# Other start addresses for the operands of the split float32 matmuls in a cross-attention and FFN block

## What is computed

```python
x = x + softmax((LN(x) @ Wq) @ (ctx @ Wk).T / 8) @ (ctx @ Wv) @ Wo + bo     # per head
xq = fake_quant(LN(x), clip_x)             # one scale for the whole tensor
gate = xq @ wq(w_gate).T                   # weights with one scale per row
up = xq @ wq(w_up).T
h = fake_quant(silu(gate) * up, clip_down) # one scale for the whole tensor
x = x + h @ wq(w_down).T
```

## Time and profile before

| | |
|---|---|
| median of three runs | 544.03 us |
| profiled execution, its own time | 544.1 us |
| span from its first to its last instruction | 542.2 us |
| PE busy | 527.4 us, 97% of the span |
| VectorE busy | 473.0 us, 87% |
| ScalarE busy | 294.3 us, 54% |
| GpSimd busy | 231.7 us, 43% |
| granted TensorE clock | 0.999, the level of 2.4 GHz |

### The profile page before, as it was taken

One profiled execution on the slowest core, in us unless ns is written; L12 is line 12 of the kernel. 1 busy time (PEld: TensorE's weight loads), 2 busy tenths in 40 slices (PEclk: granted clock), 3 DMA queues, 4 the chain that ended last, 5 costly groups with the idle time before them and its releaser, 6 DMA issues.

```text
span 542.2 us, 8065 instructions
## 1 busy us (share of the span) xinstructions
PE 527.4 (97%) x2740; PEld 356.1 (66%) x2740; DVE 473.0 (87%) x879; ACT 294.3 (54%) x414; POOL 231.7 (43%) x349
## 2 busy tenths in 40 slices
PE   8999889999999999999999899999999999999997
PEld 7878678887888878888778644444444445444444
DVE  4966888989989899898989789999999988899884
ACT  4843646555455654554534656555555633999500
POOL 4386749679596886856453000000000000055442
PEclk9999999999999999999999999999999999999999
DMA  8818365765668466445959954841342120399987
GB/s 313 280 77 292 96 192 174 252 182 187 207 216 257 158 216 186 155 131 166 209 91 316 275 154 213 317 126 21 100 117 58 60 39 13 131 324 230 157 105 129
DMA packets 82942, 93.83 MB, mean 173 GB/s; under 512 B 47085, under 2 KB 50157, under 8 KB 82645
## 3 DMA queue, kind: packets, MB, share of 16 engines
q1 hardware_dynamic: 77877, 84.13, 50.3%
q0 software_dynamic: 4320, 7.87, 9.4%
q10 hardware_dynamic: 704, 1.31, 0.8%
HBM read 47.51 MB, written 37.78 MB: 157 GB/s over the span
## 4 chain that ended last, share of the span: by engine, by line
PE 81%; DVE 9%; DMA 3%; SPq 2%; issue 2%; ACT 1%; POOL 1%; DVEq 0%; POOLq 0%
PE QO L570 14%; PE SP L575 14%; PE QO L306 5%; PE SP L371 5%; PE QO L308 5%; PE QO L307 5%; PE QO L622 4%; PE PTP L622 4%; PE SP L622 4%; PE MI L444 2%; PE MI L442 2%; PE MI L443 2%; PE PTP L404 2%; PE WOP L622 2%; PE WOP L444 2%; PE WOP L442 2%
## 5 line engine op out<-in xcount | busy, mean ns | idle before, releaser
L1489 POOL DMA_DIRECT2D out<-n2b x30 | 30.3, 1044 | 206.6 <-DVE n2b L1302 206.6
L852 ACT ACTIVATE sil<-QO,fsc 128x512 f32<-128x512 f32 x87 | 59.8, 687 | 70.1 <-PE QO L570 68.4
L570 PE MATMUL QO<-nT,wgu 128*128 128x512 bf16 x340 | 87.3, 379 | 0.1
L575 PE MATMUL SP<-nT,wgu 128*128 128x512 bf16 x340 | 87.3, 380 | 0.0
L1239 DVE SCALAR_TENSOR_TENSOR h<-SP,fsc,sil 128x512 f32<-128x512 f32 x87 | 65.1, 748 | 8.3 <-PE SP L575 6.2
L1393 POOL TENSOR_TENSOR PN<-P,rs 128x512 f32<-128x512 f32 x64 | 44.2, 712 | 49.1 <-DVE rs L935 49.1
L1245 DVE TENSOR_REDUCE hmx<-h 128x1 f32<-128x512 f32 (+1 forms) x89 | 60.1, 679 | 2.9
L575 PEld LDWEIGHTS SP<-nT,wgu 128*128 128x128 bf16 x340 | 33.2, 98 | 40.2 <-DVE h L1239 0.3
L570 PEld LDWEIGHTS QO<-nT,wgu 128*128 128x128 bf16 x340 | 33.0, 98 | 40.4 <-DMA nT<-qb 0.7
L684 ACT ACTIVATE P<-P,r 128x616 f32<-128x616 f32 x32 | 25.9, 811 | 59.6 <-DVE P L926 59.6
L306 PE MATMUL QO<-xTs,wqs 128*128 128x512 f32 x124 | 50.4, 407 | 2.1 <-DVE xTs L890 1.9
(11 more groups left out here) (223 smaller groups left out, 1202.1 us busy)
## 6 DMA issues: line engine op xcount, KB each, us to landing
xTr<-in_xT SPq DMA_DIRECT2D x8, 1024.0 KB, 8.0
xn<-in_x SPq DMA_DIRECT2D x32, 256.0 KB, 3.9
out<-x SPq DMA_DIRECT2D x32, 256.0 KB, 2.7
n_rows<-n SPq DMA_DIRECT2D x32, 256.0 KB, 2.6
n2b<-n_rows SPq DMA_DIRECT2D x32, 256.0 KB, 3.9
out<-n2b POOLq DMA_DIRECT2D x30, 256.0 KB, 6.4
h_spill<-h SPq DMA_DIRECT2D x2, 2816.0 KB, 9.4
h<-h_spill SPq DMA_DIRECT2D x6, 768.0 KB, 7.2
```

What stands on the lines that cost most here:

```text
L570: mm = e.matmul(QO[:, at:at + 512], wgu_v[:, k, cols(ic)], nT[:, b % 2, :, k, :], start=(k == 0), stop=(k == 3))
L575: mm = e.matmul(SP[:, at:at + 512], wgu_v[:, k, cols(NI + ic)], nT[:, b % 2, :, k, :], start=(k == 0), stop=(k == 3))
L852: e.activation(sil[:, n % SR, :], QO[:, (n % 2) * 512:(n % 2) * 512 + 512], ACT.Silu, scale=fsc[:, ic:ic + 1]).then_inc(silu, 1)
```

## The change

Five lines change. An unused tensor of 32 bytes goes ahead of `wqs` and shifts all that follows from 96 to 128 bytes modulo 512. The rows of `xTs` are allocated 528 elements long instead of 512 and those of `wos` 520; only the first 512 elements are used, so that the chunks stand 2112 bytes (64 modulo 512) and 2080 bytes (32 modulo 512) apart. Two more unused tensors bring `vbd`, `os` and `pts` to 128 modulo 512. No instruction is added, removed or moved; only the addresses in them differ.

```diff
+        sb(ctx, "pad", [128, 8])
         early = ExitStack()
         wqs = sb(early, "wqs", [128, 2, 4, D], f32r)
         xTr = sb(early, "xTr", [128, 4, 512])
-        xTs = sb(early, "xTs", [128, 2, 4, 512], f32r)
+        xTs = sb(early, "xTs", [128, 2, 4, 528], f32r)[:, :, :, 0:512]
         xn = sb(early, "xn", [128, XR, D])
-        wos = sb(early, "wos", [128, 2, 4, D], f32r)
+        wos = sb(early, "wos", [128, 2, 4, 520], f32r)[:, :, :, 0:D]
 ...
         late = ExitStack()
+        sb(late, "unused3", [128, 16])
         P = sb(late, "P", [128, UR, HL])
         PN = sb(late, "PN", [128, 2, 640])
         qs = sb(late, "qs", [128, 2, 4, 512])
         wint = sb(late, "wint", [128, 2, I], bf16)
-        sb(late, "unused0", [128, 8])
+        sb(late, "unused0", [128, 56])
         vbd = sb(late, "vbd", [128, 2, 5, 128], f32r)
```

## The result

The changed kernel takes 545.88 us (median of 7 runs, 545.21 to 546.51), the kernel before 544.06 us (7 runs, 543.92 to 544.64). The ratio is 1.0029 with a 95% interval of 1.002 to 1.0038. The change makes the kernel slower by 0.3%; forecast was a gain of 2.3 us. The time is inside the range, on the side of the first rival. Four executions of the kernel before, timed beside the experiments, took 674, 1396, 1920 and 1920 us and are used nowhere.

A forecast was written before the change was run, and what follows sets the result against it. PE was taken as the bound, matmul count times pace. 3 ns off each of 768 query and output matmuls, all counted, gave 544.1 minus 2.3, 541.8, or 541.7 from the median; range 538.0 to 547.8.

The forecast's parts named there:

- the first rival: Query and output projections lose their settled pace and run at the value projection's 395 ns: 3.1 us more, 547.2; chance 0.34.
- The value I take is 388: Row duration in ns forecast for 768 query and output projection matmuls, from a mean of 391: 2.3 us less.
- the chain of 390 to 398: Query and output rows after some 45 waits, up to ten slow matmuls each; a changing difference was claimed to prevent repeats.
- the key projection as the nearest case: Set-up loop with fixed weights and wandering moving data, 1 ns below the settled pace, 3 below at its shortest; supported 388.
- the upper bound: Query and output projections behaving as the value projection, 395 ns: 4 ns for 768 matmuls, 3.1 us more.
- The second rival: Addresses have no effect, and the value projection's 395 comes from short runs after waits: 544.0; chance 0.20.
- The third: All or most of the split matmuls' 11 ns surcharge vanishes in query and output projections: 9.2 us on PE, 536; chance 0.08.
- VectorE's slack: 19.5 us between 80 and 300 us, 11.8 of it waiting for the output projection's last matmul; wait shrinks when PE speeds up.
- the page's rule: PE has two independent SBUF read ports, so weight loading costs nothing; taken at its word addresses can't matter, 544.0.

The follow-up runs named there:

- number 1: Kernel before with only 32 unused bytes ahead of all split operands, which start at 128 instead of 96 modulo 512; 544.37 us, ratio 1.0001.
- Number 11: Kernel before with low parts of `xTs` and `wos` moved 256 bytes from the high parts, of `pts` 128; 544.72 us, ratio 1.0004.
- number 9: Kernel before with fixed differences of 240 (query), 48 (output), 8 bytes (values), `wks` pushed by 32; one profiled execution, 2.8 us above before's 544.1.
- number 12: Kernel before with `cts` rows 640 elements instead of 616 and `wks` at 96, giving the value projection difference 0; 544.67 us, ratio 1.0006.
- number 4: Kernel before with whole tensors pushed to fixed differences of 64 (query), 256 (output) and 32 bytes (values); 545.42 us, ratio 1.0022.
- number 2: Kernel before with only the rows of `xTs` 528 elements long, so only the query's moving data shift; 545.77 us, ratio 1.0027.

## Why the prediction was wrong

**Where the time is made.** Right: PE's pace sets the time, the whole effect lies before 300 us, the FFN lasts 146 us, and the shift to other bytes alone moved nothing (number 1, ratio 1.0001).

**The step that failed** is "The value I take is 388" for the 768 matmuls of the query and output projection. The sum took 3 ns off each, 2.3 us less; the runs showed 4.2 ns more for 384 and 1.6 ns more for 384, 2.2 us the other way. Both reasons given for 388 were wrong.

The first was that a changing difference can't repeat the chain of 390 to 398, put at some 45 waits. The chain was read as a price of the fixed difference, but it is the way into the state of 227 ns that of all the values tried only a difference of 0 modulo 256 has. Number 11 has a difference that changes from matmul to matmul and keeps both chain and lock; a query chunk of the changed kernel goes 236, 228, 232, 233, 234, 232, 233, 231, 229, 233, and its long runs go on between 225 and 241. Without the lock there is nothing that the missing chain could save. Nor was there as much to save: the query's mean is 228.1 and its settled pace 226.8, so the whole chain costs 1.3 ns in each of both loops, 1.0 us for 768, and a row of 388 ns is a pace of 225, below every settled pace measured.

The second was the key projection as the nearest case. It has the same pattern (weights fixed, moving data wandering), and it stood only 8 and 13 ns above its 308 columns. But it shows no response to the difference: its medians are 302 to 305 ns with `wks` moved 32 bytes (number 9). That alone proves little, since many differences are mixed there before and after; number 12 is plainer, because there the matmuls on the first half of `cts` have a difference of 0 and those on the second half one of 208, and the starts after them lie 141.4 and 141.2 ns on. A row that doesn't react to the thing that is varied is no measure of what varying it does. The value projection, with the right size of 512 columns and the wrong operand wandering, was the better neighbour; its 395 was put aside as the upper bound and should have been the value. Its weights wander where here the moving data do, which was held against it; in the query that made no difference.

**The first rival**, the lost lock, was right that the changed difference costs the settled pace, and right in the query's size; that any difference will do as long as it stays the same was wrong (number 4), and that the next weights are what a matmul meets wasn't tried. The numbers: 395 and 394 where 395 was said, and L307's successor passed 392.4, though L443's stayed at 390 and 391. For the output projection it said 4 ns and 1.6 came (390 to 394), where the steps of 32 bytes give another row of differences; which row of changing differences gives which pace isn't derived. An estimate by averaging the fixed values of the table gives 230.3 for the query and 231.4 for the output, and 232.0 and 229.5 were settled. Of its 3.1 us 2.2 came on PE, of which 0.9 went into idle time of PE ahead of the FFN.

**The second rival**, nothing changes, fell with the value projection of number 12, whose long run settles as soon as its difference is 0. **The third**, that the surcharge goes, fell entirely: of 14 values of the difference modulo 256 none is under 226.5 ns, where bf16 has 216.

**VectorE's slack** behaved as described. Its wait for the output projection's last matmul grew from 11.8 to 12.7 us, and PE's wait for `xTs` is gone there; a slower PE arrives later, but number 2, which is as slow, keeps most of that wait, so the reason isn't shown. Waits of VectorE between 80 and 300 us in the changed kernel (total us, times, longest):

```profile
DVE x L964 <- PE MI L446: 12.7, 6, 2.6
```

**By the page's rule**, that weight loading takes nothing from the running matmul ("TensorE: Matmul & The Clock Gate" of the Trainium skill, section "Step-by-step: what each phase is for"), all the kernels here would take the same time, as the prediction read it. The spread of 226.8 to 237.7 ns for one shape and type, by nothing but where the two reads start against each other, goes against that for split matmuls of 512 columns; for bf16 the rows agree. That the two reads meet is the nearest explanation, but no view shows the reads themselves.

**Open.** The median is 1.8 us above before's and the profiled execution 1.1; another run of the changed kernel with 545.95 us has a span of 544.1, so that the rest lies inside the span, but no trace of such a run was taken. Why the period is 256 bytes, and whether a matmul's own weights or the next one's count, wasn't tried (in these loops both start at the same residue). Differences between the values tried, and ones that aren't a multiple of 4 bytes, are unknown. Why 308 columns don't respond isn't known. The share of the extra that reaches the end varies from 0.5 to 1.1 in the table; PE's waits in the set-up differ by some tenths of a microsecond from layout to layout, and these weren't followed up.

No version beat the kernel before: the best differ from it by 0.0001 to 0.0006, within their intervals.

## What to carry to other kernels

Where PE is the bound, read its pace from the starts, per loop, and compare loops of the same shape and type: a loop that settles at its lowest pace and one that doesn't, side by side, can point to the layout. For fp32r matmuls with 512 moving columns let weights and moving data start equal modulo 256 bytes; spreading them apart costs 2 to 11 ns of 227 for each. When a bound is taken from a neighbouring row, first ask whether that row is known to respond to what is changed, and if it isn't, take the row of the same size.

## What the runs showed of the hardware

- The pace of an fp32r matmul with 512 columns depends on the difference of the two start addresses modulo 256 bytes: 227 ns at 0, 229 at 64, 231 to 236 at most others, 238 at 4. The place of both together (96 or 128) doesn't matter.
- Behind matmuls of another form, with or without a wait, a run with difference 0 needs two to eleven matmuls, with paces of 223 to 238 ns, until it stays at 227; directly behind a loop that stands at 227 it needs none (11 of 51 runs of the kernel before). With 64 bytes it ends in a cycle of 226, 229 and 232.
- The settled pace is 226.67 ns, 544 cycles at the granted 2.4 GHz, for 512 columns. In the kernel before, the starts of the settled matmuls (513 in 44 runs) fall on one common grid of 6.667 ns, 16 cycles, within 1.2 ns (the trace has whole ns); 226.67 is 34 of its steps. What has this period isn't seen in the trace.
- Matmuls of 308 columns (fp32r) stand at 141 ns at differences of 0 and of 208 alike (number 12), and the bf16 ones of 512 at 216 in every kernel.
